# Ten gathered tiles fetched row by row by SP, with the row number in a register

## The chip, the cores and the metric

The kernel runs on one core of a Trainium2 chip. The metric is the time of one execution on the device in microseconds. The core's engines are TensorE (PE), VectorE (DVE), ScalarE (ACT), GpSimd (POOL) and SyncE (SP). SP computes nothing; it issues transfers and waits on semaphores. All transfers run on the core's 16 DMA engines.

## What is computed

One layer of a graph network over 50,000 nodes and 50,000 edges, followed by a residual and a layer norm:

```python
f_s, f_v = fctp(x_s, x_v, lin1)          # per node
gs, gv = f_s[edge_src], f_v[edge_src]    # gather by the edge's source
weight = silu(edge_scalars @ fc_w1 / sqrt(8)) @ fc_w2 / sqrt(64)
edge_feat = products(gs, gv, edge_attr, weight)
mid = segment_sum(edge_feat, edge_dst, num_segments=N) / sqrt(16)
conv = fctp(mid, lin2);  angle = 0.1 * (mid_s @ lin3_w) / sqrt(96) * node_attr
out = layernorm(x + cos(angle) * fctp(x, sc) + sin(angle) * conv)
```

The kernel gathers raw node rows, applies `lin1` and `lin2` per edge, and adds the edges' results into a table `acc` in HBM.

## The kernel before

Edges are padded to 392 tiles of 128, one edge on each partition, and worked in 196 pairs. The work has two parts, one after the other.

**The edge part.** For each tile, GpSimd issues an indirect gather (`gather(n)`, L293) that brings 128 rows of 161 fp32 (644 bytes) from `xa` or, for odd tiles, from its permuted copy `x_odd` into `x_sb`, a ring of `X_RING` = 48 pairs. TensorE transposes the pair (L508) and ScalarE copies the result (L617); the linear maps and products follow over the next five loop steps of TensorE, ending in `combine`, which merges edges of one destination, and in ScalarE's copy L581 into a ring of `RING` = 48 pairs. GpSimd then adds the tile into `acc` with an indirect accumulating transfer (`scatter(t)`, L306). A scatter waits for its tile's copy, for its row numbers and for the landing of the previous scatter of the same parity.

GpSimd issues everything in one fixed order: first the gathers of 60 pairs (`AHEAD`), then 392 scatters, among which the other 272 gathers are spread evenly until 20 scatters are left. A gather into a ring place that was used before waits until TensorE has transposed its former pair (`xt_ready`) and DVE has read its attributes (`q_done`, L723).

**SP in the edge part.** It loads the indices and constants, clears `acc` (L219, until 119 us), and then waits for the transposes of all 196 pairs (L252). Only then does it load `x` for the second part (L230, L231), into the memory that the gather ring used; once all scatters have landed it loads `acc` (L239).

**The node part.** 98 groups of four tiles: self connection on TensorE, sine and cosine, sums, statistics and the norm on the other engines, stores by SP (L249).

Of the kernel before, what the change touches and what calls it, by code (L numbers as in the profile page):

```python
# [6 lines left out]
P = 128  # L7
NS, NV, MU = 64, 96, 32
ROW = NS + NV
ROWA = ROW + 1  # L10
# [6 lines left out]
X_RING = 48  # L17
GATHER_SEMS = 16
AHEAD = 60
TAIL = 10  # L20
HANDED = 2.0 ** -8
SLOTS = 4
CHUNK = 4
# [26 lines left out]
        eng.wait_ge(sem, count)  # L50


def gnn_program(nc, xa, x_odd, x_last, src, dst, dst_rows, ea4, ea8t, constants, acc, out):
    fp32, i32 = mybir.dt.float32, mybir.dt.int32
    ALU, ACT = mybir.AluOpType, mybir.ActivationFunctionType
    NT = dst.shape[1]
    NPAIR = NT // 2
    NG = NT // G
    NODES = NT * P
# [14 lines left out]
    def batch_rows(t, b):  # L74

        g, count = BATCHES[b]
        return t[g * G * P:(g + count) * G * P, :].rearrange("(p j) c -> p j c", p=P)

    ZEROS = acc.shape[0] // (SPARE * P)
    acc_z = acc.rearrange("(c p k) r -> c p (k r)", p=P, k=SPARE)  # L80

    with ExitStack() as ctx:  # L82
# [6 lines left out]
        def sem(name):  # L89
            return ctx.enter_context(nc.semaphore(name))  # L90
# [3 lines left out]
        views, column = [], 0  # L94
# [7 lines left out]
        dst_f = sb("dst_f", [P, NT])  # L102
        spare_row = sb("spare_row", [P, NT], i32)
        to_spare = sb("to_spare", [P, NT])
        ea4_sb = sb("ea4_sb", [P, NT, 4])

        src_sb = sb("src_sb", [P, NT], i32)
# [37 lines left out]
        x_sb = x_shared[:, 0:X_RING * 2 * ROWA].rearrange("p (s c) -> p s c", s=X_RING)  # L145
# [32 lines left out]
        idx_in = sem("idx_in")  # L178
        zeroed_tile = sem("zeroed_tile")
        acc_zeroed = [sem(f"acc_zeroed{s}") for s in range(ZEROING)]  # L180
        prep = sem("prep")
        weights_scaled = sem("weights_scaled")
        gathered = [sem(f"gathered{s}") for s in range(GATHER_SEMS)]
        src_in = sem("src_in")
        e8_in = [sem(f"e8_in{s}") for s in range(ROUNDS)]
        dstrow_in = [sem(f"dstrow_in{s}") for s in range(ROUNDS)]
        scattered = [sem(f"scattered{j}") for j in range(2)]
        xt_ready, z_ready, f_ready, w_ready = sem("xt_ready"), sem("z_ready"), sem("f_ready"), sem("w_ready")
# [3 lines left out]
        q_done, prod_done, feat_done = sem("q_done"), sem("prod_done"), sem("feat_done")  # L192
# [15 lines left out]
        chain = sem("chain")  # L208
        block = ctx.enter_context(nc.Block())

        @block.sync
        def _(sp):

            sp.dma_start(src_sb[:, :], src).then_inc(src_in, 16)
            sp.dma_start(constants_sb[:, :], constants).then_inc(consts, 16)
            sp.wait_ge(zeroed_tile, 1)
            for c in range(ZEROS):
                wait(sp, acc_zeroed[c % ZEROING], c // ZEROING * 16)
                sp.dma_start(acc_z[c, :, :], zeros[:, :]).then_inc(acc_zeroed[c % ZEROING], 16)  # L219
            for z in range(ZEROING):  # L220
                sp.wait_ge(acc_zeroed[z], 16 * len(range(z, ZEROS, ZEROING)))

            def load_x(b):
                g, count = BATCHES[b]
                if b >= LOADED:
                    over, groups = BATCHES[b - LOADED]
                    sp.wait_ge(x_added, over + groups)
                    sp.wait_ge(xnt_ready, over + groups)
                    sp.wait_ge(triga_done, b - LOADED + 1)
                sp.dma_start(xn_sb[:, b % LOADED, 0:count * G, :], batch_rows(xa, b)).then_inc(xn_in[b % LOADED], 16)  # L230
                sp.dma_start(xl_sb[:, b % LOADED, 0:count * P], batch_rows(x_last, b).rearrange("p j c -> p (j c)")  # L231
                             ).then_inc(xl_in[b % LOADED], 16)

            def load_acc(b):
                g, count = BATCHES[b]
                if b >= LOADED:
                    over, groups = BATCHES[b - LOADED]
                    sp.wait_ge(y_done, over + groups)
                sp.dma_start(cs_sb[:, b % LOADED, 0:count * G, :], batch_rows(acc, b)).then_inc(acc_in[b % LOADED], 16)  # L239

            def store(s):
                b = max(k for k in range(NB) if BATCHES[k][0] <= s)
                g, count = BATCHES[b]
                sp.wait_ge(norm_done, s + 1)
                if s >= TAIL_FIRST:
                    sp.wait_ge(norm_dve, s + 1 - TAIL_FIRST)
                if TAIL_FIRST <= s < TAIL_MIDDLE:
                    sp.wait_ge(norm_pool, s + 1 - TAIL_FIRST)
                sp.dma_start(batch_rows(out, b)[:, (s - g) * G:(s - g + 1) * G, :],  # L249
                             y_sb[:, s % Y_RING, :, :]).then_inc(stored[s % Y_RING], 16)  # L250

            sp.wait_ge(xt_ready, NPAIR)  # L252
            sp.wait_ge(q_done, NPAIR)
            for b in range(LOADED):
                load_x(b)
            for j in range(2):
                sp.wait_ge(scattered[j], 16 * NPAIR)
            for b in range(LOADED):
                load_acc(b)
            stores = 0  # L260
            for b in range(LOADED, NB):
                load_x(b)
                load_acc(b)
                g, count = BATCHES[b - 1]
                while stores < g - BATCH - 5:
                    store(stores)
                    stores += 1
            while stores < NG:
                store(stores)
                stores += 1  # L270
            for s in range(Y_RING):
                sp.wait_ge(stored[s], 16 * len(range(s, NG, Y_RING)))

        @block.gpsimd
        def _(pool):
# [6 lines left out]

            def gather(n):

                g, j = n // 2, n % 2
                sem_at, slot = g % GATHER_SEMS, g % X_RING
                if j == 0:
                    if g >= X_RING:
                        pool.wait_ge(xt_ready, g - X_RING + 1)
                        pool.wait_ge(q_done, g - X_RING + 1)  # L290
                    if g >= GATHER_SEMS:
                        pool.wait_ge(gathered[sem_at], g // GATHER_SEMS * 32)
                pool.indirect_dma_start(  # L293
                    out=x_sb[:, slot, j * ROWA:(j + 1) * ROWA], out_offset=None, in_=(xa, x_odd)[j],
                    in_offset=bass.IndirectOffsetOnAxis(ap=src_sb[:, n:n + 1], axis=0),
                ).then_inc(gathered[sem_at], 16)

            def scatter(t):
# [15 lines left out]
            for z in range(ZEROING):  # L314
                pool.wait_ge(acc_zeroed[z], 16 * len(range(z, ZEROS, ZEROING)))

            left, over = NT - 2 * AHEAD, NT - 2 * TAIL
            for t in range(NT):
                scatter(t)
                if t < over:  # L320
# [118 lines left out]
        def _(pe):  # L439
# [19 lines left out]
            for k in range(-1, NPAIR + 4):  # L459
                e, d, c, a = k - 4, k - 2, k - 1, k + 1  # L460
# [38 lines left out]
                if a < NPAIR:  # L499
                    chunk = a // CHUNK  # L500
                    pe.wait_ge(e8_in[chunk % ROUNDS], (chunk // ROUNDS + 1) * 16)
                    wait(pe, h_done, a)
                    nc.tensor.matmul(Z[:, 0:P], fc_w1_sb[:, :], e8_sb[:, chunk % ROUNDS, a % CHUNK, :],
                                     start=True, stop=True).then_inc(z_ready, 1)
                    pe.wait_ge(gathered[a % GATHER_SEMS], (a // GATHER_SEMS + 1) * 32)
                    wait(pe, xt_copied, a)
                    for b, column in enumerate((1, ROWA + ROW - P, 1 + P)):
                        last = nc.tensor.transpose(XT[:, b * P:(b + 1) * P], x_sb[:, a % X_RING, column:column + P],  # L508
                                                   ident_sb[:, :])
                    last.then_inc(xt_ready, 1)  # L510
# [35 lines left out]
            for b in range(NB):  # L546
                g, count = BATCHES[b]
# [124 lines left out]
        def _(dve):  # L672
# [17 lines left out]
            nc.vector.tensor_copy(dst_f[:, :], dst_i[:, :]).then_inc(chain, 1)  # L690
            dve.wait_ge(chain, 3)
            dve.wait_ge(prep, 3)
            nc.vector.tensor_tensor(to_spare[:, :], spare_row[:, :], dst_f[:, :], ALU.subtract).then_inc(chain, 1)
            dve.wait_ge(chain, 4)

            for k in range(NPAIR + 3):
                d = k - 3
                if d >= 0:
# [11 lines left out]
                    for j in range(2):  # L710
                        r = d % CHUNK * 2 + j
# [7 lines left out]
                                            vq_sb[:, :, :, :].rearrange("p j c o -> p j (c o)"),  # L719
                                            ALU.add).then_inc(feat_done, 1)  # L720
                if k < NPAIR:
                    dve.wait_ge(gathered[k % GATHER_SEMS], (k // GATHER_SEMS + 1) * 32)
                    nc.vector.tensor_tensor(q_sb[:, k % SLOTS, :, :], ea4_sb[:, 2 * k:2 * k + 2, :],  # L723
                                            x_sb[:, k % X_RING, 0:2 * ROWA:2 * ROWA - 1].rearrange(
                                                "p (j o) -> p j o", o=1).to_broadcast([P, 2, 4]),
                                            ALU.mult).then_inc(q_done, 1)
# [186 lines left out]
def layouts(x, src, dst, edge_attr_4, edge_attr_8, node_vec1, sc_w0, sc_w1, lin1_w0, lin1_w1, fc_w1,  # L913
# [45 lines left out]
    def two_tiles(w):  # L959
# [24 lines left out]

        "x_last": np.ascontiguousarray(xa[:, 1 + P:]),
        "src": src_p.reshape(P, tiles),
        "dst": dst_p.reshape(P, tiles),
        "dst_rows": np.concatenate([dst_p.reshape(P, tiles).T, np.full((1, P), -1, np.int32)]),
        "ea4": ea4.reshape(P, tiles, 4),
# [25 lines left out]
```

## Time and profile before

| | us |
|---|---|
| median of 3 runs | 1653.58 (1653.57 to 1654.6) |
| the profiled execution's own time | 1655.28 |
| its span, first to last instruction | 1653.4 |
| mean granted clock of TensorE, share of full | 0.909 |

PE, DVE, ACT and POOL below are the engines named above; PEld is TensorE's weight load; SPq and ACTq are the queues on which these two issue transfers, and a duration there is the time that an issue took. L12 is line 12 of the kernel. "Idle before" is what an engine stood still before an instruction, with what released it; "issue" there means that the profile shows nothing it waited for. Pairs count from 0, so the copy of pair 32 is the 33rd instruction of L617.

### The profile page before, as it was taken

To read this page: it belongs to the slowest core of one execution; us is meant where nothing else is said; L and a number is where in the kernel's file an instruction comes from. 1 tells how busy PE (TensorE), PEld (TensorE's weight loads), DVE (VectorE), ACT (ScalarE), POOL (GpSimd) and SP (SyncE) were. 2 spreads that over 40 slices of the span, in tenths; PEclk is the share of its full clock that TensorE was granted. 3 is DMA by queue.
4 is the path that set the end of the run, shared out by engine and by line. 5 is a ranking of instruction groups with operands and counts; after the bars stand their busy time and mean duration, and the time that the engine had idled before them with its cause. 6 is when DMAs were issued, how large, how long until landed. Compare 5 with 4: busy or idle time off the path is not lost. (4 is left out here: it accounts for less than half of the span.)

```text
span 1653.4 us, 28910 instructions
## 1 busy us (share of the span) xinstructions
PE 1296.2 (78%) x8524; PEld 1138.1 (69%) x8524; DVE 925.5 (56%) x4542; ACT 816.2 (49%) x1880; POOL 1320.0 (80%) x1190
## 2 busy tenths in 40 slices
PE   6999999999997777777867777777677177777773
PEld 5888888888886666666756676666666066666652
DVE  4777777777774344444453444444443077777776
ACT  3666666666663333343333334343333027777775
POOL 7777778887877777788887888777775588899985
PEclk9999999999999778898898888788989589999997
DMA  9993444444544444444444444444446569888854
GB/s 371 380 375 102 85 80 82 81 80 79 90 84 65 63 67 77 64 65 80 65 66 77 66 67 69 74 64 65 81 61 168 137 255 342 324 327 322 322 207 159
DMA packets 114761, 235.19 MB, mean 142 GB/s; under 512 B 17264, under 2 KB 77232, under 8 KB 111024
## 3 DMA queue, kind: packets, MB, share of 16 engines
q0 software_dynamic: 75264, 64.68, 28.2%
q1 hardware_dynamic: 28080, 137.15, 21.3%
q10 hardware_dynamic: 11264, 31.52, 5.9%
q8 instruction: 72, 1.18, 0.3%
q14 instruction: 81, 0.66, 0.1%
HBM read 135.88 MB, written 97.40 MB: 141 GB/s over the span
## 5 line engine op out<-in xcount | busy, mean ns | idle before, releaser
L306 POOL DMA_INDIRECT acc<-shared,row_sb x392 | 624.6, 1593 | 156.2 <-issue 97.6
L739 DVE TENSOR_TENSOR shared<-shared 128x192 f32<-128x192 f32 x196 | 70.5, 360 | 558.5 <-ACT shared L609 558.5
L508 PE MATMUL XTZ<-constants_sb,x_shared 128*128 128x128 f32 x588 | 118.0, 314 | 206.6 <-DMA x_shared<-x_odd,src_sb 203.7
L293 POOL DMA_INDIRECT x_shared<-xa,src_sb x196 | 202.7, 1034 | 60.3 <-issue 47.3
L293 POOL DMA_INDIRECT x_shared<-x_odd,src_sb x196 | 198.8, 1014 | 59.8 <-issue 49.1
L468 PE MATMUL OC<-constants_sb,shared 128*128 128x193 f32 x784 | 230.6, 380 | 0.0
L508 PEld LDWEIGHTS XTZ<-constants_sb,x_shared 128*128 128x128 f32 x588 | 66.3, 151 | 236.3 <-DMA x_shared<-x_odd,src_sb 222.4
L617 ACT COPY shared<-XTZ 128x384 f32<-128x384 f32 x196 | 93.9, 479 | 262.3 <-PE XTZ L508 262.3
L451 PE MATMUL OC<-shared 128*128 128x161 f32 x784 | 198.0, 337 | 2.8 <-ACT shared L581 2.1
L581 ACT ACTIVATE shared<-OC,is_last 128x161 f32<-128x161 f32 x392 | 155.3, 396 | 71.1 <-PE OC L455 39.6
L455 PE MATMUL OC<-shared 128*128 128x161 f32 x782 | 189.9, 328 | 0.0
L596 ACT COPY shared<-OC 128x386 f32<-128x386 f32 x196 | 94.4, 482 | 175.5 <-PE OC L470 174.1
L647 ACT ACTIVATE shared<-shared,shift,rstd_mean 128x160 f32<-128x160 f32 x364 | 159.8, 518 | 32.4 <-DVE shift L838 32.4
L712 DVE SCALAR_TENSOR_TENSOR shared<-dstrow_sb,dst_f,constants_sb 128x256 f32<-128x256 int32 x392 | 173.2, 478 | 0.0
L470 PEld LDWEIGHTS OC<-constants_sb,shared 128*128 128x128 f32 x784 | 164.4, 221 | 0.0
L470 PE MATMUL OC<-constants_sb,shared 128*128 128x97 f32 x784 | 158.8, 289 | 0.0
L496 PE MATMUL W<-constants_sb,shared 64*128 64x192 f32 x784 | 157.8, 351 | 0.0
L468 PEld LDWEIGHTS OC<-constants_sb,shared 128*128 128x128 f32 x784 | 146.4, 223 | 0.0
L455 PEld LDWEIGHTS OC<-shared 128*128 128x128 f32 x782 | 145.2, 213 | 0.0
L487 PE MATMUL FPT<-constants_sb,shared 128*128 128x160 f32 x784 | 140.6, 302 | 0.6 <-ACT shared L617 0.6
L451 PEld LDWEIGHTS OC<-shared 128*128 128x128 f32 x784 | 134.3, 214 | 4.2 <-issue 1.8
L400 POOL TENSOR_TENSOR shared<-shared,x_shared 128x640 f32<-128x640 f32 x98 | 129.6, 1323 | 0.0
(92 smaller groups left out, 2713.3 us busy)
## 6 DMA issues: line engine op xcount, KB each, us to landing
acc<-xnt_zeros SPq DMA_DIRECT2D x50, 644.0 KB, 6.5
out<-shared SPq DMA_DIRECT2D x98, 320.0 KB, 9.4
x_shared<-xa SPq DMA_DIRECT2D x13, 2254.0 KB, 8.9
shared<-acc SPq DMA_DIRECT2D x13, 2254.0 KB, 15.1
dstrow_sb<-dst_rows ACTq DMA_DIRECT2D x49, 576.0 KB, 4.1
acc<-shared,row_sb POOLq DMA_INDIRECT x392
x_shared<-x_last SPq DMA_DIRECT2D x13, 448.0 KB, 9.3
x_shared<-xa,src_sb POOLq DMA_INDIRECT x196, 2.7
```

Of the source, the lines that this page charges most:

```text
L293: pool.indirect_dma_start(out=x_sb[:, slot, j * ROWA:(j + 1) * ROWA], out_offset=None, in_=(xa, x_odd)[j], in_offset=bass.IndirectOffsetOn ...
L306: pool.indirect_dma_start(out=acc, out_offset=bass.IndirectOffsetOnAxis(ap=row_sb[:, t:t + 1], axis=0), in_=comb_sb[:, k % RING, j, :], in ...
L451: last = nc.tensor.matmul(out_rows, same_sb[:, e % SLOTS, j, 0:P], feat_sb[:, e % SLOTS, j, 0:ROWA], start=True, stop=t == 0)
L455: last = nc.tensor.matmul(out_rows, same_sb[:, b % SLOTS, i, P:2 * P], comb_sb[:, b % RING, i, :], start=False, stop=True)
L468: nc.tensor.matmul(OUT[:, o:o + OUTW], pt_sb[:, d % 2, (2 + j) * P:(3 + j) * P], lin2_b_sb[:, :], start=True, stop=False)
L470: last = nc.tensor.matmul(OUT[:, o + NV:o + OUTW], pt_sb[:, d % 2, j * P:(j + 1) * P], lin2_a_sb[:, :], start=False, stop=True)
L487: nc.tensor.matmul(F[:, j * ROW:(j + 1) * ROW], xt_sb[:, k % 2, j * P:(j + 1) * P], lin1_a_sb[:, :], start=j == 0, stop=False)
L496: last = nc.tensor.matmul(W[:, j, 0:NW], h_sb[j * NS:(j + 1) * NS, k % 2, :], fc_w2_sb[j * NS:(j + 1) * NS, :], start=True, stop=True)
L508: last = nc.tensor.transpose(XT[:, b * P:(b + 1) * P], x_sb[:, a % X_RING, column:column + P], ident_sb[:, :])
L581: nc.scalar.activation(comb_sb[:, e % RING, j, :], COMB[:, j * ROWA:(j + 1) * ROWA], ACT.Copy, scale=is_last[:, t:t + 1]).then_inc(comb_co ...
L647: last = nc.scalar.activation(y[:, j, :], y[:, j, :], ACT.Identity, bias=shift[:, k % STAGED, n:n + 1], scale=rstd_mean[:, k % STAGED, 0, ...
L712: last = nc.vector.scalar_tensor_tensor(same_sb[:, d % SLOTS, j, :], dstrow_sb[:, chunk % ROUNDS, r:r + 2, :].rearrange("p b e -> p (b e)" ...
```

## The change

Pairs 80, 108, 136, 164 and 192 (ten tiles) are taken out of GpSimd's gathers. For each of their 1280 rows SP loads the row number from SBUF into a register and issues one direct transfer of that row, with the address from the register. All of them count on one semaphore for each pair, and TensorE and DVE wait on it for these pairs. GpSimd's 382 other gathers are renumbered over the 16 semaphores, and 262 instead of 272 are spread among the scatters. SP brings the row numbers of a tile (512 bytes) into row 0 of `spare_row`, after DVE has read that tile (`spare_read`), one tile ahead. SP's fetches stand in its program between the clearing of `acc` and the wait of L252.

```diff
-            nc.vector.tensor_tensor(to_spare[:, :], spare_row[:, :], dst_f[:, :], ALU.subtract).then_inc(chain, 1)
-            dve.wait_ge(chain, 4)
+            nc.vector.tensor_tensor(to_spare[:, :], spare_row[:, :], dst_f[:, :], ALU.subtract).then_inc(spare_read, 1)
+            dve.wait_ge(spare_read, 1)
@@ helpers
+SP_FIRST, SP_STEP, SP_COUNT = 80, 28, 5
+    SP_PAIRS = [SP_FIRST + SP_STEP * n for n in range(SP_COUNT)]
+    POOL_PAIRS = [g for g in range(NPAIR) if g not in SP_PAIRS]
+    def wait_gathered(eng, g):
+        if g in SP_PAIRS:
+            eng.wait_ge(sp_gathered[SP_PAIRS.index(g)], 2 * P * 16)
+        else:
+            n = POOL_PAIRS.index(g)
+            eng.wait_ge(gathered[n % GATHER_SEMS], (n // GATHER_SEMS + 1) * 32)
@@ SP, after the clearing of acc
+            def load_indices(t):
+                r = t % 3
+                sp.dma_start(spare_row[0:1, r * P:(r + 1) * P], src_rows[:, t * P:(t + 1) * P]).then_inc(rows_in[r], 16)
+            def gather_rows(t):
+                n, j, r = t // 2, t % 2, t % 3
+                g = SP_PAIRS[n]
+                if t + 1 < 2 * SP_COUNT:
+                    load_indices(t + 1)
+                sp.wait_ge(xt_ready, g - X_RING + 1)
+                sp.wait_ge(q_done, g - X_RING + 1)
+                sp.wait_ge(rows_in[r], (t // 3 + 1) * 16)
+                for p in range(P):
+                    row = sp.value_load(spare_row[0:1, r * P + p:r * P + p + 1], min_val=0, max_val=NODES - 1)
+                    sp.dma_start(x_sb[p:p + 1, g % X_RING, j * ROWA:(j + 1) * ROWA], (xa, x_odd)[j][bass.ds(row, 1), :]
+                                 ).then_inc(sp_gathered[n], 16)
+            sp.wait_ge(spare_read, 1)
+            load_indices(0)
+            for t in range(2 * SP_COUNT):
+                gather_rows(t)
@@ GpSimd
-                g, j = n // 2, n % 2
-                sem_at, slot = g % GATHER_SEMS, g % X_RING
+                g, j = POOL_PAIRS[n // 2], n % 2
+                sem_at, slot, column = n // 2 % GATHER_SEMS, g % X_RING, 2 * g + j
-            left, over = NT - 2 * AHEAD, NT - 2 * TAIL
+            left, over = 2 * len(POOL_PAIRS) - 2 * AHEAD, NT - 2 * TAIL
@@ TensorE and DVE
-                    pe.wait_ge(gathered[a % GATHER_SEMS], (a // GATHER_SEMS + 1) * 32)
+                    wait_gathered(pe, a)
-                    dve.wait_ge(gathered[k % GATHER_SEMS], (k // GATHER_SEMS + 1) * 32)
+                    wait_gathered(dve, k)
```

## Rows read from the trace of the kernel before

**Rows 1.** Profile page: busy us, share of span, instructions.
```profile
PE 1296.2 (78%) x8524; PEld 1138.1 (69%) x8524; DVE 925.5 (56%) x4542; ACT 816.2 (49%) x1880; POOL 1320.0 (80%) x1190
```

**Rows 2.** Busy time by stretch: length, then each engine with its count, granted clock, DMA.
```profile
500.00:1250.00 750.00, 546.40 (x3257) 491.80 (x3257) 323.38 (x1680) 283.01 (x651) 599.74 (x442) 0.86 0.44 68
153.00:500.00 347.00, 345.89 (x2517) 308.53 (x2516) 249.08 (x1301) 219.05 (x504) 278.83 (x205) 1.00 0.48 82
...
1310.00:1653.00 343.00, 242.90 (x1639) 196.78 (x1639) 242.91 (x1000) 217.82 (x506) 291.44 (x398) 0.91 0.74 284
```

**Rows 3.** Costliest groups 500 to 1250 us: busy, mean ns, idle before and releasers.
```profile
L306 POOL DMA_INDIRECT acc<-shared,row_sb x255 | 405.7, 1591 | 93.5 <-issue 62.7 <-DMA acc<-shared,row_sb 11.4 <-ACT shared L581 10.8
...
L293 POOL DMA_INDIRECT x_shared<-xa,src_sb x94 | 99.7, 1061 | 28.7 <-issue 19.8 <-DMA acc<-shared,row_sb 6.4 <-PE XTZ L508 2.1
L293 POOL DMA_INDIRECT x_shared<-x_odd,src_sb x93 | 95.5, 1026 | 28.4 <-issue 20.7 <-DMA acc<-shared,row_sb 7.0 <-ACT shared L581 0.6
```

**Rows 4.** Waits 400 to 1150 us, PE then POOL: total us, times, longest.
```profile
PE XTZ L508 <- DMA x_shared<-x_odd,src_sb: 171.5, 67, 4.1
...
POOL acc L306 <- DMA acc<-shared,row_sb: 10.9, 12, 1.5
```

**Rows 5.** Timeline of GpSimd at its last gathers: start, duration, instruction, idle before.
```profile
1252.28 1.02 POOL L293 DMA_INDIRECT x_shared<-x_odd,src_sb  x1 [0.30 <-DMA acc<-shared,row_sb]
...
1266.76 1.56 POOL L306 DMA_INDIRECT acc<-shared,row_sb  x1 [3.38 <-DMA acc<-shared,row_sb]
1274.43 1.55 POOL L306 DMA_INDIRECT acc<-shared,row_sb  x1 [6.10 <-DMA acc<-shared,row_sb]
...
1303.88 1.55 POOL L306 DMA_INDIRECT acc<-shared,row_sb  x1 [0.49 <-issue]
```

**Rows 6.** Timeline of SP's queue: start, time the issue took, transfer.
```profile
1256.38 0.33 SPq L230 DMA_DIRECT2D x_shared<-xa  x1
1256.76 0.43 SPq L231 DMA_DIRECT2D x_shared<-x_last  x1
1257.23 0.43 SPq L230 DMA_DIRECT2D x_shared<-xa  x1
...
1307.39 1.28 SPq L239 DMA_DIRECT2D shared<-acc  x3
```

**Rows 7.** Timeline of ScalarE, copies of pairs 32, 80, 108, 192, 195 and last L581.
```profile
165.72 0.48 ACT L617 COPY shared<-XTZ 128x384 f32<-128x384 f32 x1 [0.20 <-PE XTZ L508]
...
396.72 0.48 ACT L617 COPY shared<-XTZ 128x384 f32<-128x384 f32 x1 [0.20 <-PE XTZ L508]
...
557.18 0.48 ACT L617 COPY shared<-XTZ 128x384 f32<-128x384 f32 x1 [4.16 <-PE XTZ L508]
...
1232.91 0.48 ACT L617 COPY shared<-XTZ 128x384 f32<-128x384 f32 x1 [0.20 <-PE XTZ L508]
...
1255.62 0.48 ACT L617 COPY shared<-XTZ 128x384 f32<-128x384 f32 x1 [2.16 <-PE XTZ L508]
...
1270.85 0.40 ACT L581 ACTIVATE shared<-OC,is_last 128x161 f32<-128x161 f32 x1 [0.90 <-PE OC L455]
```

**Rows 8.** Scatters issued (L306) up to the copies of pairs 108 and 192.
```profile
0.00:557.18 557.18, 218.15 (x136) 0.99 0.59 148
0.00:1232.91 1232.91, 583.84 (x366) 0.92 0.51 104
```

**Rows 9.** Tiles combined (L581) up to the same two moments.
```profile
0.00:557.18 557.18, 82.42 (x208) 0.99 0.59 148
0.00:1232.91 1232.91, 148.98 (x376) 0.92 0.51 104
```

**Rows 10.** Waits of SP's queue: total us, times, longest.
```profile
SPq L252 <- PE XTZ L508: 1136.7, 1, 1136.7
```

**Rows 11.** Chain that ended last, in time order: start, length, what.
```profile
1635.50 0.07 issue
```

**Rows 12.** Line L293, transfer from issue to landing.
```profile
DMA to landing us min/median/max: 2.5/2.8/8.3
```

More of the change, by code:

```diff
@@ L50, in wait, with gnn_program @@
         eng.wait_ge(sem, count)
-def gnn_program(nc, xa, x_odd, x_last, src, dst, dst_rows, ea4, ea8t, constants, acc, out):
+def gnn_program(nc, xa, x_odd, x_last, src, src_rows, dst, dst_rows, ea4, ea8t, constants, acc, out):
     fp32, i32 = mybir.dt.float32, mybir.dt.int32
@@ L180, in gnn_program @@
         acc_zeroed = [sem(f"acc_zeroed{s}") for s in range(ZEROING)]
-        prep = sem("prep")
+        prep, spare_read = sem("prep"), sem("spare_read")
         weights_scaled = sem("weights_scaled")
         gathered = [sem(f"gathered{s}") for s in range(GATHER_SEMS)]
+        sp_gathered = [sem(f"sp_gathered{n}") for n in range(SP_COUNT)]
         src_in = sem("src_in")
+        rows_in = [sem(f"rows_in{r}") for r in range(3)]
         e8_in = [sem(f"e8_in{s}") for s in range(ROUNDS)]
@@ L290, in gather @@
                         pool.wait_ge(q_done, g - X_RING + 1)
-                    if g >= GATHER_SEMS:
-                        pool.wait_ge(gathered[sem_at], g // GATHER_SEMS * 32)
+                    if n // 2 >= GATHER_SEMS:
+                        pool.wait_ge(gathered[sem_at], n // 2 // GATHER_SEMS * 32)
                 pool.indirect_dma_start(
                     out=x_sb[:, slot, j * ROWA:(j + 1) * ROWA], out_offset=None, in_=(xa, x_odd)[j],
-                    in_offset=bass.IndirectOffsetOnAxis(ap=src_sb[:, n:n + 1], axis=0),
+                    in_offset=bass.IndirectOffsetOnAxis(ap=src_sb[:, column:column + 1], axis=0),
                 ).then_inc(gathered[sem_at], 16)
@@ L986, in layouts @@
         "src": src_p.reshape(P, tiles),
+        "src_rows": np.ascontiguousarray(src_p.reshape(P, tiles // 2, 2)[:, SP_FIRST:SP_FIRST + SP_STEP * SP_COUNT:SP_STEP, :]
+                                         .transpose(1, 2, 0)).reshape(1, SP_COUNT * 2 * P),
         "dst": dst_p.reshape(P, tiles),
```

## The prediction

> **What bounds the kernel now.** I read the busy shares first, then the stretches, then the waits of the engines that could be the bound. Over the whole span POOL (80%) and PE (78%) look alike [rows 1], which decides nothing; the stretches do [rows 2]. From 153 to 500 us PE is busy for 345.89 of 347 us and bounds. From 500 to 1250 us it is busy for 546 of 750 and its granted clock falls to 0.86, while POOL carries 599.74 us of work. The groups of that stretch show how [rows 3]: 255 scatters of 1.591 us with 93.5 us of idle before them and 187 gathers of 1.044 us (99.7 + 95.5 over 94 + 93) with 57.1 before them; together 405.7 + 93.5 + 195.2 + 57.1 = 751.5 us. So POOL's queue is full without a hole, and nearly all of its idle is "issue", the turn from one transfer to the next. PE's waits say the same from the other side: 171.5 us for the gathered rows of `x_odd`, in waits of at most 4.1 us [rows 4]. The queue also has a backlog: when pair 192 is copied, 376 tiles are combined and 366 scattered; at pair 108 it was 208 against 136 [rows 8, 9]. Thus every microsecond taken from POOL's queue before its last scatter (issued at 1303.88 [rows 5]) brings the end of the edge part forward, whichever engine bounds at the moment when it is taken, as long as a backlog stands. After that last scatter SP loads `acc` at 1307.39 [rows 6], and the node part runs to 1653.4. It holds no gather and moves as a block.
>
> **What is removed.** Ten gathers, each 1.044 us busy and 57.1 / 187 = 0.305 us of turn [rows 3]: 10 x 1.349 = 13.5 us. All ten stood before the last gather at 1252.28 [rows 5]. A part comes back. A scatter waits for the landing of the last one but one, and POOL already waits 10.9 us for that in 750 us [rows 4], 11.4 in the stretch of 442 transfers [rows 3]. Ten more places without a gather between two scatters leave ten landings less cover. At 11.4 / 255 = 0.045 us for each scatter this is 0.4 us; if each of the ten places cost the largest wait there, 1.5 us, the whole gain would go. I take 0.1 us each, 1 us in all, near the mean. Net: -12.5 us. It is not less than nothing: POOL has fewer instructions and no new wait, as SP's pairs are left out of its order.
>
> **What is added to SP.** SP has been idle in the edge part: it waits 1136.7 us in one piece for the transposes (L252) [rows 10]. The fetches fill this hole, and what is queued behind them is L252 and the loads of `x`. The question is whether 1280 rows fit in it, in time for the pairs that need them. Start: pair 80 may overwrite the ring place of pair 32 once that is transposed, at 165.5 [rows 7]; the clearing of `acc` and the first row numbers are over before. After it no gate is near: pair 108 needs pair 60. Deadlines today: pairs 80, 108 and 192 are copied at 396.72, 557.18 and 1232.91 [rows 7]. They must be landed some 3 us earlier (2.8 us is the median of a gather's rows [rows 12]).
>
> Late rows do not cost at once, for POOL lives on its backlog. At pair 108 that is 72 tiles [rows 8, 9]; a scatter with its share of gathers takes 751.5 / 255 = 2.9 us, so PE may stand still for some 200 us there and catch up later, at the 4.8 us a pair of the PE-bound stretch (pairs 32 to 80 take 231 us) against 8.0 today (pairs 108 to 192 take 675.7). The last pair decides. From its copy at 1232.91 today to the last combined tile are 38 us, but 15.2 of these lie behind the copy of pair 195 (1255.62 to 1270.85) [rows 7] and three pairs at PE's own pace are 14.4. So if pair 192 lands at time L, the last tile is combined at L + 1 + 14.4 + 15.2 and the last scatter lands some 5 us on (1.6 to issue it, 3 to land): L + 36. With the gain the edge part would end at 1307.4 - 13.5 = 1293.9. So no loss while L is under 1258, and with L = 165.5 + 1280 R + 3 the row price R may be up to **0.85 us**. At 0.86 the gain is gone; above it each further 0.01 us costs 12.8 us.
>
> **The price of a row.** It is one register load with its address work, and one direct issue. The issue: SP starts transfers 0.38 and 0.47 us apart when nothing stands between them [rows 6]; these are of 128 partitions, one row may be less. I take 0.42. The load: no row of this trace shows one. From below, 0.07 us is what an engine's queue takes between two dependent small instructions [rows 11]. From above, a register load as dear as a whole direct issue is 0.47. Between them is the turn of POOL's queue from one transfer to the next, 0.30 us [rows 5], in which a queue does its own bookkeeping; I take that, for a row as a whole is just this, bookkeeping and an issue. R = 0.42 + 0.30 = **0.72**, ends 0.45 and 0.94. At 0.72 SP ends pair 192 at 165.5 + 922 = 1087, 130 us early; pair 108 (512 rows) is there at 534 + 3, before 557; pair 80 (256 rows) at 350, before 397.
>
> The Trainium skill speaks against the change here. Its page DMA: Bandwidth & Descriptors, section Latency and other measured facts, gives a `tensor_load` a floor of about 600 ns. No run or row here shows one yet. Beside 0.42 that would be a row of 1.02 us, and by the sum above an end some 215 us later than without loss. Its page Runtime: NRT & Kernel Launch, section Instruction fetch mechanics, gives about 200 ns for each register loaded from HBM; that would be 0.62 us a row and no loss. The two pages disagree on the sign.
>
> **What else moves.** The ten loads of 512 bytes of row numbers are ten issues of 0.4 us, one tile ahead, and hidden by the tile before. About four row transfers are in flight at once (2.8 us to land, one issued each 0.72), where six of the far larger loads of `x` are issued without a stop [rows 6]. The bytes are the same as before on another queue; the DMA engines are at 0.44 of their time in this stretch [rows 2], so I cost it at nothing. If that cover were gone, scatters would land later and the 1 us above would grow. The renumbered semaphores of POOL's gathers change nothing in time. `spare_read` lets DVE wait as before. The loads of `x` follow the last transposes as now, 13 us earlier, and hit the last scatters as now (waits of 3.38 and 6.10 us [rows 5]).
>
> **The rivals.**
> A. SP keeps up, the forecast: span 1653.4 - 12.5 = 1640.9. The profiled execution's own time, 1655.28, is 1.7 above the median 1653.58; against the median the forecast is **1641.1 us**, with 1638 to 1646 of its own (give-back of 0 to 5, and a gather priced at its median).
> B. SP is late: a row costs more than 0.86 us. Its place is the wait of TensorE for pair 192, after which nothing is left in POOL's backlog. For it: the load is unpriced, and the margin from 0.72 to 0.86 is thinner than the load itself. Against it: the same queue turns and issues in under 0.5 us. At R = 0.94, the upper end, L = 1371.7 and the edge part ends at 1407.7, 114 us beyond 1293.9: 1754 us. If the load takes twice POOL's turn, 0.60, R is 1.02 and the time 1641 + 216 = 1857; at R = 1.05 it is 1895. This is the case in which the first page's rule holds.
> C. SP is late by far: two instructions more, for bounds or for the address, as dear as an issue each (R = 1.36): 165.5 + 1741 + 39 = 1945, 651 us beyond, some 2290.
> D. The change does not do what it says: POOL is relieved but its scatters then wait for landings, because nothing is between them (1.5 us for each place [rows 4]), or small row transfers delay them. The gain of 13.5 shrinks to 3 or less: 1651 to 1655.
>
> **How the numbers follow.** A 0.58, B 0.25, C 0.10, D 0.07. Two parts in a hundred of B's are rows around 0.85 with a small gain or none. A change under 0.2% (3.3 us) cannot be told from none. Faster: A, and a little of D, 0.60. Same: most of D and the narrow pass of B at 0.86, 0.06. Slower: 0.34. The range starts at 1637 (all of 13.5 us and a little) and must reach into B; to 1900, R = 1.05, only C and the last of B are out, some 0.14.
>
> **What would show it.** L293 has 382 gathers and POOL's stretch to the last scatter is 13 us shorter with the same turns of 0.30. SP's queue shows 1280 direct transfers, whose spacing is R; the wait at L252 is still long (some 130 us) if A holds, and absent if B or C does. TensorE's wait for pairs 80 to 192 names a transfer of SP's if B holds: first at pair 80 (beyond 0.89 us a row) or pair 108 (beyond 0.76), where lateness costs nothing, and at 192 in hundreds of microseconds. A spacing above 0.86 us makes the forecast wrong, whatever POOL gains.

## The result, and the profile after

| | us |
|---|---|
| before, median of 4 runs | 1653.57 (1650.07 to 1654.6) |
| changed kernel, median of 4 runs | 2202.74 (2185.48 to 2209.05) |
| ratio | 1.331, 95% interval 1.3225 to 1.3394 |
| the profiled execution's own time, and its span | 2197.23, 2195.4 |

The changed kernel is 549 us slower. That lies outside the predicted range of 1637 to 1900; of the cases it is nearest to C, which had a chance of 0.10 and a price of 2290.

The page of the changed kernel, parts 1 and 2: busy us with share of the span and instructions, then the span in 40 slices of 55 us.

```profile
PE 1211.2 (55%) x8524; PEld 1059.7 (48%) x8524; DVE 923.3 (42%) x4542; ACT 815.1 (37%) x1880; POOL 1305.7 (59%) x1180
...
POOL 7778788887878607780007870008860014898986
PEclk9999999659985559975559975559975556999998
```

POOL has 1305.7 us of work against 1320.0 before [rows 1]: the relief of some 14 us is real. But its busy digits now fall to 0 in four places, and TensorE's granted clock (last line) falls with them, to 5 tenths in the emptiest slices. Somebody is waited for. The waits of TensorE say who (total us, times, longest; before: [rows 4]):

```profile
PE XTZ L546 <- DMA x_shared<-x_odd: 852.1, 5, 189.2
```

Five waits, one for each pair that SP fetches, 852 us in all. For GpSimd's gathers TensorE waits 0.5 us in the whole run, where it was 203.7 us before. These 203.7 us, and some 104 us of the first wait, which cost nothing (see below), make up about the difference between the 852 us of waits and the 549 us lost. What SP does in that time is seen in the two lines of the fetch loop. L252 is the load of the row number, L253 the transfer; the columns are count, ns min/median/max, first and last start in us.

```profile
L252 SPq TENSOR_LOAD <-spare_row x1280: 426/478/715, 170.5 to 1795.6; - x183
L252 SPq FUSED_REGOPS  x1280: 152/152/181, 171.0 to 1796.1; - x183
L252 SPq SEQ_ASSERT  x1280: 18/18/33, 171.2 to 1796.3; - x183
```

```profile
L253 SPq FUSED_REGOPS  x1280: 42/42/42, 171.3 to 1796.4; - x183
L253 SPq MOVE x_shared<-xa x640: 29/29/29, 171.4 to 1635.3; - x160
L253 SPq DMA_DIRECT2D x_shared<-xa x640: 269/270/289, 171.5 to 1635.4; - x160
L253 SPq MOVE x_shared<-x_odd x640: 29/29/29, 335.5 to 1796.5; - x160
L253 SPq DMA_DIRECT2D x_shared<-x_odd x640: 269/270/273, 335.6 to 1796.6; - x160
```

A row is not two instructions but six: the register load 0.478 us, two for the bounds (`FUSED_REGOPS` 0.152 and `SEQ_ASSERT` 0.018 of L252, which are gone in experiment 6), two for the address (0.042 and 0.029), and the issue 0.270. They add up to 0.989 us. From the first issue (171.5) to the last (1796.6) are 1279 rows, 1.271 us each; so the six turns between the instructions take the other 0.28, some 0.047 each. The last pair lands at about 1797; TensorE goes on at 1797.79. SP's queue then shows the end of the edge part, as in [rows 6]:

```profile
1790.34 6.48 SPq L253 DMA_DIRECT2D x_shared<-x_odd  x6
1817.70 0.37 SPq L268 DMA_DIRECT2D x_shared<-xa  x1
...
1850.00 1.28 SPq L277 DMA_DIRECT2D shared<-acc  x3
```

The load of `acc` is issued at 1850.0 instead of 1307.39, and from there to the end are 345.4 us, where [rows 6] with the span gives 346.0. So the 542.0 us between the two spans all lie before that load, which is issued 542.6 us later.

The backlog can be followed too. Tiles scattered (L344) and tiles combined (L619) up to six moments; the count in brackets is the column to read, as in [rows 8, 9]. The moments are the start of a wait of TensorE and its end, for pairs 80, 108 and 136.

```profile
0.00:394.04 394.04, 130.79 (x82) 1.00 0.64 176
0.00:498.00 498.00, 189.15 (x119) 0.90 0.59 151
0.00:630.00 630.00, 260.81 (x164) 0.92 0.57 136
0.00:824.00 824.00, 329.91 (x208) 0.83 0.50 113
0.00:957.00 957.00, 400.49 (x253) 0.85 0.49 108
0.00:1149.00 1149.00, 419.14 (x264) 0.79 0.43 92
```

```profile
0.00:394.04 394.04, 59.32 (x150) 1.00 0.64 176
0.00:498.00 498.00, 60.11 (x152) 0.90 0.59 151
0.00:630.00 630.00, 81.46 (x206) 0.92 0.57 136
0.00:824.00 824.00, 82.25 (x208) 0.83 0.50 113
0.00:957.00 957.00, 103.60 (x262) 0.85 0.49 108
0.00:1149.00 1149.00, 104.39 (x264) 0.79 0.43 92
```

During the first wait POOL goes on: it scatters 37 tiles while TensorE finishes 2, and its lag shrinks from 68 tiles to 33. The second wait, 189 us, uses up the rest: 208 are combined, 208 scattered. From there on POOL has next to nothing to live on (9 tiles at the start of the third wait, none at its end), and the waits of TensorE are waits of the kernel.

### The profile page after: what moved, and what is told of

Its sections match the earlier page's. It is cut to its first block and busy times, and to the rows that moved or that the text cites. A ratio compares the mean times of both kernels' runs of the same rounds, so it can differ in the third digit from the quotient of the medians.

```text
span 2195.4 us, 36598 instructions
## 1 busy us (share of the span) xinstructions
PE 1211.2 (55%) x8524; PEld 1059.7 (48%) x8524; DVE 923.3 (42%) x4542; ACT 815.1 (37%) x1880; POOL 1305.7 (59%) x1180
## 3 DMA queue, kind: packets, MB, share of 16 engines
q1 hardware_dynamic: 30660, 137.99, 16.3%
## 5 line engine op out<-in xcount | busy, mean ns | idle before, releaser
L344 POOL DMA_INDIRECT acc<-shared,row_sb x392 | 621.9, 1587 | 715.7 <-ACT shared L619 347.4
L546 PE MATMUL XTZ<-constants_sb,x_shared 128*128 128x128 f32 x588 | 110.1, 297 | 852.6 <-DMA x_shared<-x_odd 852.1
L761 DVE TENSOR_TENSOR shared<-ea_sb,x_shared 128x8 f32<-128x8 f32 x196 | 31.2, 159 | 837.0 <-DMA x_shared<-x_odd 836.6
L331 POOL DMA_INDIRECT x_shared<-xa,src_sb x191 | 195.2, 1022 | 58.8 <-issue 43.9
L506 PE MATMUL OC<-constants_sb,shared 128*128 128x193 f32 x784 | 201.9, 340 | 0.0
L489 PE MATMUL OC<-shared 128*128 128x161 f32 x784 | 180.2, 312 | 2.8 <-ACT shared L619 2.1
L493 PE MATMUL OC<-shared 128*128 128x161 f32 x782 | 173.0, 303 | 0.0
L619 ACT ACTIVATE shared<-OC,is_last 128x161 f32<-128x161 f32 x392 | 155.0, 395 | 41.7 <-PE OC L493 10.1
L508 PE MATMUL OC<-constants_sb,shared 128*128 128x97 f32 x784 | 142.9, 265 | 0.0
L508 PEld LDWEIGHTS OC<-constants_sb,shared 128*128 128x128 f32 x784 | 141.8, 194 | 0.0
L493 PEld LDWEIGHTS OC<-shared 128*128 128x128 f32 x782 | 129.8, 193 | 0.0
L506 PEld LDWEIGHTS OC<-constants_sb,shared 128*128 128x128 f32 x784 | 126.3, 195 | 0.0
```

The lines of the kernel that those rows point to most:

```text
L331: pool.indirect_dma_start(out=x_sb[:, slot, j * ROWA:(j + 1) * ROWA], out_offset=None, in_=(xa, x_odd)[j], in_offset=bass.IndirectOffsetOn ...
L344: pool.indirect_dma_start(out=acc, out_offset=bass.IndirectOffsetOnAxis(ap=row_sb[:, t:t + 1], axis=0), in_=comb_sb[:, k % RING, j, :], in ...
L489: last = nc.tensor.matmul(out_rows, same_sb[:, e % SLOTS, j, 0:P], feat_sb[:, e % SLOTS, j, 0:ROWA], start=True, stop=t == 0)
L493: last = nc.tensor.matmul(out_rows, same_sb[:, b % SLOTS, i, P:2 * P], comb_sb[:, b % RING, i, :], start=False, stop=True)
L506: nc.tensor.matmul(OUT[:, o:o + OUTW], pt_sb[:, d % 2, (2 + j) * P:(3 + j) * P], lin2_b_sb[:, :], start=True, stop=False)
L508: last = nc.tensor.matmul(OUT[:, o + NV:o + OUTW], pt_sb[:, d % 2, j * P:(j + 1) * P], lin2_a_sb[:, :], start=False, stop=True)
```

## The experiments

All times are medians; each ratio is against runs of the kernel before on the same chip, taken alongside, whose medians were 1652.2 to 1653.8. The number in brackets behind a ratio is its 95% interval.

**1. Is it the instructions of SP, or the small transfers?** The 1280 transfers stay, the register is taken away. The fixed rows are not the edges' rows, so the result of ten tiles differs.

```diff
-    row = sp.value_load(spare_row[0:1, r * P + p:r * P + p + 1], min_val=0, max_val=NODES - 1)
-    sp.dma_start(x_sb[p:p + 1, ...], (xa, x_odd)[j][bass.ds(row, 1), :]).then_inc(sp_gathered[n], 16)
+    sp.dma_start(x_sb[p:p + 1, ...], (xa, x_odd)[j][t * P + p:t * P + p + 1, :]).then_inc(sp_gathered[n], 16)
```

> The changed kernel, its 1280 single-row transfers kept, but each from a fixed row of the table, so without register load and address work (the ten tiles get wrong rows; the timing of everything else stays). In the changed kernel a row takes 1.27 us on SP: 0.478 register load, 0.152 + 0.018 bounds, 0.042 + 0.029 address, 0.270 issue, and gaps. Theory 1 (SP's instructions for a row set the pace): a row now takes 0.27 + gap = about 0.32 us, pair 192 is there by 165 + 410 = 575 us, no pair is waited for, and POOL's relief of 13.5 us shows: about 1641 us. Rival (the small transfers themselves are slow, landing or queue): rows stay above 1 us apart and the time near 2200. Rival (relief is given back in scatter waits): 1651 to 1655.

Measured: 1641.13 us (1634.62 to 1647.31), ratio 0.9927 (0.9905 to 0.9949). The line of the transfers, and SP's wait for a free ring place (L250: total us, times, longest):

```profile
L252 SPq DMA_DIRECT2D x_shared<-xa x640: 222/252/712, 168.2 to 878.6; - x160
L252 SPq DMA_DIRECT2D x_shared<-x_odd x640: 222/252/427, 207.0 to 916.7; - x160
```

```profile
SPq L250 <- DVE shared L760: 405.8, 5, 144.7
```

The first tile is issued in 207.0 - 168.2 = 38.8 us, 0.30 us a row, and SP now waits for ring places, not TensorE for SP. So 1280 single-row transfers do no harm (from fixed rows here; experiment 5 shows the same with the edges' own rows); what costs is what stands before each of them in SP's program. With SP out of the way the kernel takes what case A of the prediction gave, 1641.1.

**2. One load for eight rows.** Same work, same result, with the bounds kept.

```diff
-    row = sp.value_load(spare_row[0:1, r * P + p:r * P + p + 1], min_val=0, max_val=NODES - 1)
+    _, rows = nc.values_load_multi_w_load_instructions(      # once for 8 rows
+        spare_row[0:1, r * P + q:r * P + q + 8], engines=[mybir.EngineType.SP], min_val=0, max_val=NODES - 1)
     ...                                                      # the transfers of the 8 rows follow
```

> The changed kernel with one register load for eight row numbers in place of one load for each; no bounds instructions are built for it. Nothing is left out. Theory 1: a row costs (0.48 to 0.9) / 8 + 0.07 address + 0.27 issue + gaps = 0.45 to 0.55 us, the last pair is there by 165 + 1280 x 0.55 = 870 us, no waits for SP's pairs: about 1641 us. If the load costs 0.478 for each register, the row stays near 0.95 us (without the bounds), late by 1280 x (0.95 - 0.85) = 128 us: about 1770.

Measured: 1636.37 us (1633.51 to 1638.43), ratio 0.9912 (0.989 to 0.9933). The expectation was right in the time and wrong in one step: it said that no bounds instructions would be left, and there are 1280 of each of the two. So its price of 0.45 to 0.55 us a row was too low as well.

```profile
L252 SPq FUSED_REGOPS  x1280: 147/147/181, 171.7 to 1175.7; - x183
L252 SPq SEQ_ASSERT  x1280: 18/18/33, 172.0 to 1175.9; - x183
L252 SPq TENSOR_LOAD <-spare_row x160: 687/778/965, 171.0 to 1172.8; - x160
```

```profile
L256 SPq DMA_DIRECT2D x_shared<-xa x640: 224/225/293, 174.4 to 1078.4; - x160
...
L256 SPq DMA_DIRECT2D x_shared<-x_odd x640: 224/225/273, 275.4 to 1179.0; - x160
```

A load of eight registers takes 0.778 us, 0.097 a row instead of 0.478. The first tile takes 275.4 - 174.4 = 101 us, so R, the time SP takes for a row, is 0.79. TensorE waits twice for SP (24.3 us, of which 22.5 in one), and nothing is lost.

**3. Is a late pair a loss?** Only pair 80 by SP, at the old 1.27 us a row.

```diff
-SP_FIRST, SP_STEP, SP_COUNT = 80, 28, 5
+SP_FIRST, SP_STEP, SP_COUNT = 80, 28, 1
```

> The changed kernel with only pair 80 fetched by SP, at the same 1.27 us a row. It lands at about 499 us, 100 us after TensorE asks for it, as in the changed kernel. Theory 1 (POOL bounds and has a backlog of scatters; TensorE catches up at 4.8 us a pair against 8): the wait of 100 us costs nothing and POOL's relief of 2.7 us remains: about 1651 us. Rival (a late pair shifts all that follows): 1653.6 + 100 = about 1750 us. In between, if the backlog of some 36 pairs runs out before the end.

Measured: 1643.31 us (1639.09 to 1644.74), ratio 0.9956 (0.9939 to 0.9972).

```profile
PE XTZ L546 <- DMA x_shared<-x_odd,src_sb: 120.6, 49, 4.5
PE XTZ L546 <- DMA x_shared<-x_odd: 99.4, 1, 99.4
```

TensorE waits 99.4 us in one piece, and the kernel is faster than before. The rival (+100 us) is out: the wait is paid from the backlog, and TensorE waits less for POOL in small pieces later (120.6 us in the whole run, where it was 203.7 before). That it gained 10 us where two gathers are worth 2.7 was expected by neither, and led to experiments 7, 9 and 10.

**4. Three pairs.**

```diff
-SP_FIRST, SP_STEP, SP_COUNT = 80, 28, 5
+SP_FIRST, SP_STEP, SP_COUNT = 80, 54, 3
```

> Three pairs by SP (80, 134, 188) at 1.27 us a row: they land at about 499, 824 and 1149 us; pairs 80 and 134 are late by some 100 and 60 us, 188 is early by 50. Theory 1: only the last pair decides, so no loss, and 3 x 2.7 = 8.1 us of relief: about 1645.5 us. Rival (lateness adds up): 1800 us.

Measured: 1642.38 us (1640.0 to 1645.39), ratio 0.995 (0.9929 to 0.9971).

```profile
PE XTZ L546 <- DMA x_shared<-x_odd: 231.0, 3, 100.2
PE XTZ L546 <- DMA x_shared<-x_odd,src_sb: 45.0, 19, 4.2
```

SP delays TensorE by 231 us in three waits and the kernel still gains. But the forecast of its parts was off: pair 188 was late too. SP ended the third pair's rows at 1219.3 and not at 1149, so it began them at 1219 - 256 x 1.27 = 894. SP had ended pair 80 at 499 and could have been at pair 188 by 824. The gates held it back (SP waits 114.7 us for ring places in three waits, of which 45.0 in the longest one; in the changed kernel it is one wait of 44.9): pair 134 may start only when pair 86 is transposed, pair 188 when pair 140 is, and TensorE, held up by the pair before, came late to both. That feedback was not in the sum.

**5 and 6. The threshold.** The same two forms without the bounds instructions: one load for eight rows, and one load for each row.

```diff
+    ..., skip_runtime_bounds_check_because="..."
```

> As the kernel with one load for eight row numbers (0.79 us a row measured, 1636.4 us), but without the bounds instructions (0.147 + 0.018 us a row). A row then costs 0.778/8 + 0.037 + 0.029 + 0.225 + three gaps of 0.047 = 0.53 us. Theory 1 (below 0.85 us a row SP's pace has no effect on the end): the time stays at 1636 to 1641. Rival (SP's pace still shows, as the 22.5 us wait for pair 108 vanishes): some 5 to 20 us faster than 1636.

Measured: 1639.71 us (1638.56 to 1641.39), ratio 0.9929 (0.9908 to 0.995). R inside a tile is 0.53. No wait of TensorE for SP's rows is left, and the time is no better than at R = 0.79: the two intervals, 0.9908 to 0.995 and 0.989 to 0.9933, overlap. The rival is out.

> As the changed kernel, one load for each row, but without the bounds instructions. A row costs 0.478 + 0.042 + 0.029 + 0.270 + four gaps of 0.047 = 1.01 us instead of 1.27. Theory 1 (end of edge part = 165.5 + 1280 R + 39 us, the prediction's sum): 1508 against 1294 without loss, so 1641 + 205 = 1846, with R at 0.97 some 1795. Rival (a late pair costs more than its lateness, because the gathers or scatters behind it lose their backlog again each time): above 1900.

Measured: 1823.11 us (1821.82 to 1832.52), ratio 1.1054 (1.1018 to 1.1091).

```profile
L252 SPq TENSOR_LOAD <-spare_row x1280: 426/486/752, 167.9 to 1420.5; - x183
```

```profile
L256 SPq DMA_DIRECT2D x_shared<-xa x640: 264/265/288, 168.6 to 1296.5; - x160
...
L256 SPq DMA_DIRECT2D x_shared<-x_odd x640: 264/265/266, 294.8 to 1421.2; - x160
```

From 168.6 to 1421.2 are 1279 rows of 0.979 us. By the expectation's own sum that price gives 165.5 + 1253 + 39 = 1457.5, 164 us beyond 1294, and 1805; the other 18 us are the tail, measured in the section on why the prediction was wrong. The rival (above 1900) is out. Four kernels with the same five pairs and the same results can now be set side by side:

| us a row | 0.53 | 0.79 | 0.979 | 1.271 |
|---|---|---|---|---|
| time, us | 1639.7 | 1636.4 | 1823.1 | 2202.7 |

Between the first two the time does not rise. Between the last two, it is 379.6 us for 1280 x 0.292 = 373.8 us of SP's time: one to one. No run lies between 0.79 and 0.979, so the place of the bend is an estimate: extended down to 1641 with 1.0 for the slope, the line meets the flat part at 0.979 - 182 / 1280 = 0.84 us a row. The prediction had put the threshold at 0.85.

**7 and 8. POOL's relief by itself.** The gathers of one pair, and of all five, left out altogether, with nothing on SP; TensorE and DVE take what lies in the ring, so the results of these tiles differ. The run of one pair has `SP_COUNT` = 1 besides, as in experiment 3.

```diff
         if g in SP_PAIRS:
-            eng.wait_ge(sp_gathered[SP_PAIRS.index(g)], 2 * P * 16)
+            return
@@ SP
-            sp.wait_ge(spare_read, 1)
-            load_indices(0)
-            for t in range(2 * SP_COUNT):
-                gather_rows(t)
```

> The kernel before with the two gathers of pair 80 left out altogether (TensorE and DVE take what lies in the ring place); nothing added to SP. The kernel that fetched pair 80 by SP and let TensorE wait 99 us for it came to 1643.3 against 1653.7, 10 us less where the two gathers are worth 2.7. Theory 1 (two gathers are worth 2.7 us and the other 7 come from TensorE's pause): about 1651. Rival (the 7 come from the new spread of 270 gathers among the scatters, not from the pause): about 1643.

> The kernel before with the ten gathers of the five pairs left out altogether, nothing added to SP: POOL's relief by itself. Theory 1 (the relief is 10 x 1.35 us less 1, and SP's small transfers cost nothing): 1641, the same as with fixed rows fetched by SP (1641.1). Rival (SP's 1280 transfers slow scatters or gathers, and the relief is larger than seen): 1630 to 1636.

Measured: one pair 1643.28 us (1637.11 to 1653.76), ratio 0.9953 (0.993 to 0.9975); five pairs 1639.48 us (1634.67 to 1640.01), ratio 0.9916 (0.989 to 0.9941). With five dropped the time is that of fixed rows fetched by SP, within the scatter of the runs: no cost of SP's transfers is seen. With one dropped it is that of experiment 3, so TensorE's pause is not what gained there. By the medians the first pair brings 9 us and the next four 4 us. The two intervals overlap, so that the later pairs bring less is not shown; that one pair brings more than its 2.7 us is (its interval ends at 4 us of gain).

**9 and 10. The spread, with all gathers kept.** All tiles gathered by POOL, nothing left out, only the head longer, so that the gathers fall among the scatters as in 7 (270 over 372) and as in 8 (262 over 372).

```diff
-AHEAD = 60
+AHEAD = 61      # experiment 10: 65
```

> The kernel before with nothing left out and nothing on SP; only the head of gathers is 61 pairs long instead of 60, so that 270 gathers instead of 272 are spread over the 372 scatters, the spread that the kernel with one pair dropped has. POOL issues as many transfers as before. Theory 1 (the gain beyond 2.7 us of the kernel with one pair dropped, 1643.3 against 1652.2, comes from how the gathers fall among the scatters): about 1646. Rival (it comes from the dropped work): no change, about 1652.

> The same with a head of 65 pairs: 262 gathers spread over 372 scatters, the spread of the changed kernel, with all ten tiles still gathered by POOL. Theory 1 (the spread matters by itself): if the spread gives some 6 us, 1646, and the ten tiles' relief in the kernel with five pairs dropped (1639.5) is 7 us rather than 13.5. Rival (all of the 12.7 us there is dropped work): about 1652.

Measured: 1649.56 us (1642.75 to 1651.31), ratio 0.9963 (0.9948 to 0.9978), and 1648.29 us (1642.12 to 1654.08), ratio 0.9968 (0.9953 to 0.9984). Both are faster than before with the same number of transfers, by 4.2 and 5.5 us of the medians. This does not isolate the spread: the longer head also puts the first scatter off, from 157.5 us to 160.2 and 170.1. If the gain is that of the new spread and holds in the other kernels too, the ten gathers by themselves are worth 1648.3 - 1639.5 = 8.8 us, or 12.7 - 5.5 = 7.2 with each run against its own kernel before, and not 12.5. What brings it isn't settled. The profiles of the two show less idle before the scatters; here 153 to 1310 us of experiment 10, where the whole kernel before had 156.2 (29.4 of it for landings, 17.5 for ScalarE):

```profile
L306 POOL DMA_INDIRECT acc<-shared,row_sb x392 | 624.7, 1594 | 148.5 <-issue 103.4 <-DMA acc<-shared,row_sb 29.1 <-ACT shared L581 8.8
```

But the runs of one such kernel lie up to 12 us apart, and one profile of each can't carry a difference of 5. The profile of experiment 8, where ten gathers are gone, has as much idle before the scatters as the kernel before:

```profile
L339 POOL DMA_INDIRECT acc<-shared,row_sb x392 | 625.0, 1594 | 155.3 <-issue 93.6 <-DMA acc<-shared,row_sb 33.4 <-ACT shared L614 13.8
```

**11 and 12. More pairs.** One load for eight rows without bounds and seven pairs; one load for sixteen and eight pairs.

```diff
-SP_FIRST, SP_STEP, SP_COUNT = 80, 28, 5
+SP_FIRST, SP_STEP, SP_COUNT = 66, 20, 7      # experiment 12: 62, 18, 8
```

> Seven pairs by SP (66, 86, .. 186), one load for eight row numbers and no bounds instructions, 0.53 us a row inside a tile. The last pair is there by about 125 + 1792 x 0.55 = 1110 us, before TensorE asks for it. Theory 1 (POOL bounds, each gather taken off is worth 1.35 us): 4 tiles more than with five pairs, 5.4 us less than 1637 to 1640: about 1633. Rival (relief saturates: one pair and five pairs dropped gave 1643 and 1639): about 1638.

> Eight pairs by SP (62, 80, .. 188), one load for sixteen row numbers, no bounds instructions. If the load grows by 0.04 us for each further register (0.478 for one, 0.778 for eight), it takes 1.12 us, 0.07 a row, and a row 0.50 us: last pair by 125 + 2048 x 0.5 = 1150 us, in time. Theory 1: 16 gathers less, 2.7 us below seven pairs, about 1631. Rival (saturation): about 1638.

Measured: seven pairs 1632.42 us (1630.59 to 1638.14), ratio 0.9881 (0.9861 to 0.9901), the fastest of all; eight pairs 1633.97 us (1632.93 to 1637.49), ratio 0.989 (0.987 to 0.9909). The median of the first is that of theory 1 (1633), and its rival (1638) lies just outside the interval, which overlaps that of five pairs in experiment 2. The second gives nothing more; its median lies between theory 1 and the rival, and the two are not told apart. SP is no longer always in time there: its load takes 1.232 us for sixteen registers where 1.12 was expected, and TensorE waits for SP four times.

```profile
L252 SPq TENSOR_LOAD <-spare_row x128: 1142/1232/1488, 125.9 to 1144.3; - x128
```

```profile
PE XTZ L549 <- DMA x_shared<-x_odd: 74.4, 4, 29.5
```

## Why the prediction was wrong, point by point

**What bounds the kernel: right.** POOL's queue fills the edge part, TensorE has slack, and POOL lives on a backlog. Experiments 3 and 4 show it: 99 and 231 us of waiting for SP, and no loss.

**The relief of 12.5 us: right in sum, its parts not shown.** Experiments 1 and 8 gave 1641.1 and 1639.5 for 1641.1. That the first agrees to the decimal is luck: its runs lie from 1634.6 to 1647.3. Some 4 to 6 us of the sum may come with the new spread or the longer head of experiments 9 and 10, which the prediction didn't price; the gathers alone would then bring 7 to 9 us, and the give-back, set at 1 us, would be 5 to 6. The profiles show no such give-back: the idle before the scatters is 156.2 us before and 155.3 in experiment 8, the waits for landings among it 29.4 and 33.4. So this stays open.

**The threshold of 0.85 us a row: near, with a tail too short.** The estimate from the runs is 0.84. The prediction let the edge part end 36 us after the last pair lands; it is 1850.0 - 1797 = 53 us. Of these, 33.6 run to the last combined tile at 1830.56, where the prediction had 30.6. The other 19.4 it had as 5: it let the last scatter go out as soon as its tile was combined. But six scatters still stood in POOL's queue at 1830.56. The last eight tiles had come 1.3 to 1.9 us apart, and POOL had stood still before three scatters after SP issued the loads of `x` at 1817.70:

```profile
1823.37 1.73 POOL L344 DMA_INDIRECT acc<-shared,row_sb  x1 [3.12 <-ACT shared L619]
1828.30 1.55 POOL L344 DMA_INDIRECT acc<-shared,row_sb  x1 [3.21 <-ACT shared L619]
1835.95 1.55 POOL L344 DMA_INDIRECT acc<-shared,row_sb  x1 [6.09 <-DMA acc<-shared,row_sb]
...
1846.48 1.55 POOL L344 DMA_INDIRECT acc<-shared,row_sb  x1 [0.31 <-issue]
```

The kernel before has waits of this size at the same place (3.38 and 6.10 us [rows 5]). The prediction named them, but they are only in its end without loss (1293.9), not in its 36 us. That the loads of `x` cause them is argued from the time, not tested. With 53 us the sum gives 0.84.

**The price of a row: this is the step that failed.** It was put at 0.42 + 0.30 = 0.72 us, ends 0.45 and 0.94; it is 1.271. With only this price put right, the prediction's own sum gives 1641 + 1280 x (1.271 - 0.85) = some 2180 us, against 2202.74 measured. Three things went into the error.
- *The count.* The step priced "one register load with its address work, and one direct issue". The queue runs six instructions for these two lines of source. The four that were not counted take 0.152 + 0.018 + 0.042 + 0.029 = 0.24 us, and the turns 0.28. Two more instructions had been thought of only in case C, as a mishap, and C's sum does not follow from its words: two instructions as dear as an issue each make 0.72 + 0.84 = 1.56 us, not 1.36. That C came nearest is partly luck.
- *The stand-in.* The load was priced by POOL's turn between two transfers, 0.30, because both are a queue's bookkeeping. It isn't the same work: that row contains no read of SBUF into a register. The load's own upper end, 0.47, was within 2% of the 0.478 measured. Even that end, with the rest uncounted, left the row at 0.94; experiment 6, without the bounds, has 0.979.
- *The choice.* By the prediction's own sum the time is flat below 0.85 and rises by 12.8 us for each 0.01 above it, as the runs then showed. A price that no row shows, with ends on both sides of such a point, is no basis for calling the flat side the likely one.

The Trainium skill's figure of about 600 ns for a `tensor_load` (DMA: Bandwidth & Descriptors, Latency and other measured facts) is above the 0.478 us measured for one register, and the measurement decides. But it was nearer than the stand-in and put the row on the right side of the threshold. The page adds that the compiler unrolls by four to spread this cost. No run here unrolls single loads, but loads of several registers show that the cost can be spread: 0.478 us for one register, 0.778 for eight, 1.232 for sixteen. The other figure, 200 ns a register (Runtime: NRT & Kernel Launch, Instruction fetch mechanics), is for registers loaded from HBM; one register from SBUF took more than twice that here.

**Rival B's place** was right: TensorE's wait for SP's pairs. Its expectation that lateness at pair 108 costs nothing holds for one wait of 99 us, not for the second: after 99 and 189 us the backlog was empty. Put in, the measured row gives 1641 + 1280 x (1.271 - 0.84) = 2193, against 2202.74, or 2197.23 for the profiled execution.

## What to carry to other kernels

Before work is moved to an idle queue, count what that queue will issue for one item, instruction by instruction and with the turns between them, and hold items x price against the time at which the last one is needed: an idle engine is no proof of a fast one. A price that no row shows, on both sides of a threshold, should be measured first, by a run of a few items. Where such a queue is the limit, the first thing to change is the fixed cost for each item; here one load for eight rows turned +549 us into -17. Below the threshold a still cheaper row gains nothing: 0.53 us a row was no faster than 0.79. A late input costs nothing while the bounding engine has a backlog, and everything once it is used up, so the backlog should be read off before the lateness is called harmless.

## What the runs showed that was not expected

- A register load on SP is mostly fixed cost: 0.478 us for one register, 0.778 for eight, 1.232 for sixteen, so by estimate some 0.43 us and 0.04 to 0.06 for each register.
- A direct transfer of one row (644 bytes) is issued in 0.225 to 0.270 us, where the loads of `x`, over 128 partitions, took 0.33 to 0.43 [rows 6]. It is two packets on the mean: SP's queue has 30660 of them against 28080 before, 2580 more for 1290 transfers.
- Bounds on a value in a register cost 0.15 + 0.02 us each time, with their turns a fifth of the row of 1.271 us.
- The same number of transfers, with a longer head of gathers and fewer of them among the scatters, came out 4 to 6 us of 1650 faster. Why is open.
